# The order of the output projection and the product with the values in each pair step of a fused decoder layer

## What is computed

```python
x = x + attn(layernorm(x), Wq, Wk, Wv, Wr)            # 16 heads of 64, causal penalty -50, scale 1/8
x = x + xattn(layernorm(x), ctx, w_q, w_k, w_v, w_o)  # 16 heads of 64, no mask
x = x + ffn(layernorm(x), ...)                        # swiglu, 8 experts in 2 groups, top 2, and a shared part

# both attentions, per batch row:
scores = einsum('bqhd,bkhd->bhqk', q, k) * scale      # 128 x 128 per head
attn = softmax(scores)
out = einsum('bhqk,bkhd->bqhd', attn, v).reshape(b, s, 1024) @ W_out
```

## Time and profile before

| what | value |
|---|---|
| three timed runs | 966.55, 967.46, 970.04 us; median 967.46 |
| profiled execution, span from the first to the last instruction | 963.6 us |
| TensorE matmuls busy | 932.5 us, 97% |
| TensorE weight loads busy | 806.1 us, 84% |
| VectorE busy | 687.5 us, 71% |
| ScalarE busy | 586.6 us, 61% |
| GpSimd busy | 233.3 us, 24% |
| mean granted clock of TensorE | 0.996 |
| the attention steps (first S to the end of the last step) | 21.9 to about 654 us |

### The profile page before, as it was taken

How to read it: one execution, slowest core, us unless ns; L and a number is a source line. 1 busy time by engine, 2 the same in 40 slices (tenths; PEclk the granted TensorE clock), 3 DMA queues, 4 the chain that set the end, 5 groups by cost and what they waited for, 6 DMA issues and landing times. The chain is left out here.

```text
span 963.6 us, 17001 instructions
## 1 busy us (share of the span) xinstructions
PE 932.5 (97%) x5474; PEld 806.1 (84%) x5474; DVE 687.5 (71%) x1822; ACT 586.6 (61%) x1795; POOL 233.3 (24%) x245
## 2 busy tenths in 40 slices
PE   7999989989999999999999999998899999999998
PEld 6798878878898888888889988986788888888887
DVE  6898878778789878778878877885943554554453
ACT  4988778777788878878878887886501400400400
POOL 1443124214123434422422341344100000000000
PEclk9999999999999999999999999999999999999999
DMA  7300000000001020000000020111100000000000
GB/s 222 107 23 2 1 1 0 0 1 0 0 1 45 23 66 2 1 22 1 0 22 0 0 87 0 44 45 55 56 12 12 0 11 11 0 11 11 1 12 11
DMA packets 13193, 22.12 MB, mean 23 GB/s; under 512 B 1108, under 2 KB 7764, under 8 KB 12628
## 3 DMA queue, kind: packets, MB, share of 16 engines
q1 hardware_dynamic: 13140, 21.51, 6.8%
HBM read 19.41 MB, written 2.10 MB: 22 GB/s over the span
## 5 line engine op out<-in xcount | busy, mean ns | idle before, releaser
L385 POOL TENSOR_TENSOR prob<-prob,rsum 128x512 f32<-128x512 f32 x128 | 133.2, 1040 | 421.1 <-DVE rsum L585 421.1
L466 ACT ACTIVATE prob<-psS,nmin 128x128 f32<-128x128 f32 x512 | 180.9, 370 | 23.3 <-DVE nmin L569 15.9
L554 DVE TENSOR_TENSOR oT_lo<-psT,oT_hi 64x256 fp32r<-64x256 f32 x256 | 108.2, 422 | 16.4 <-ACT oT_hi L454 6.0
L466 ACT ACTIVATION_READ_ACCUMULATOR prob<-psS,nmin 128x1 f32 x512 | 106.5, 208 | 0.0
L448 ACT ACTIVATE pT_hi<-psT 128x512 fp32r<-128x512 f32 x128 | 71.2, 597 | 52.9 <-PE psT L723 52.1
L454 ACT ACTIVATE oT_hi<-psT 64x256 fp32r<-64x256 f32 x256 | 96.6, 377 | 8.5 <-PE psT L124 3.8
L535 DVE TENSOR_TENSOR kd_lo<-psW,kd_hi 64x512 fp32r<-64x512 f32 x128 | 88.0, 687 | 10.4 <-ACT kd_hi L437 6.9
L437 ACT ACTIVATE kd_hi<-psW 64x512 fp32r<-64x512 f32 x128 | 75.9, 593 | 16.4 <-PE psW L124 14.2
L122 PE MATMUL psT<-pT_lo,v_hi 128*128 128x256 f32 x256 | 73.6, 288 | 10.2 <-DVE pT_lo L547 10.1
L547 DVE TENSOR_TENSOR pT_lo<-psT,pT_hi 128x512 fp32r<-128x512 f32 x128 | 82.2, 682 | 1.0 <-ACT pT_hi L448 0.7
L122 PE MATMUL psS<-kd_lo,q_hi 128*128 128x256 f32 x256 | 75.0, 293 | 2.1 <-ACT prob L466 1.1
(11 more groups left out here) (198 smaller groups left out, 2616.4 us busy)
## 6 DMA issues: line engine op xcount, KB each, us to landing
stage<-w SPq DMA_DIRECT2D x4, 1024.0 KB, 4.8
stage<-ctxT SPq DMA_DIRECT2D x4, 512.0 KB, 4.1
out<-fin SPq DMA_DIRECT2D x16, 128.0 KB, 1.7
xres<-x SPq DMA_DIRECT2D x3, 512.0 KB, 8.3
stage<-wq SPq DMA_DIRECT2D x2, 512.0 KB, 5.6
stage<-wk SPq DMA_DIRECT2D x2, 512.0 KB, 6.8
stage<-wv SPq DMA_DIRECT2D x2, 512.0 KB, 5.8
stage<-wr SPq DMA_DIRECT2D x2, 512.0 KB, 4.9
```

Of the source, the lines that this page charges most:

```text
L385: nc.gpsimd.tensor_tensor(prob[:, r, :], prob[:, r, :], rsum[:, r].unsqueeze(2).broadcast_to([P, TPG, P]), ALU.mult).then_inc(prob_done, 1)
L466: e = nc.scalar.activation(prob[:, n, :], flat(psS[:])[:, n * P:(n + 1) * P], ACT.Exp, bias=nmin[:, n:n + 1], scale=-1.0, accum_out=psums[ ...
L554: nc.vector.tensor_tensor(oT[1][r, parity, b, :], banks(psT)[r, b, h, :], oT[0][r, parity, b, :].bitcast(F32), ALU.subtract).then_inc(oT_l ...
```

## The change

The two blocks of calls change places in TensorE's `step`, each with its waits. Nothing else is changed, and no other engine's program.

```diff
@@ -758,12 +758,6 @@
                         pe.wait_ge(gate_in, 32)
                         pe.wait_ge(g_lo, 1)
                         gate_logits(pe, 0)
-                    if depth > 0:
-                        if j == 1:
-                            pe.wait_ge(v_lo, G * 2 * TPG + TPG)
-                        if j == HP + 1:
-                            pe.wait_ge(v_lo, G * 2 * TPG + 2 * TPG)
-                        weighted_values(s, (j - 1) % PAIRS)
                     if depth > 1:
                         if j == 2:
                             pe.wait_ge(res_done, G + 1)
@@ -771,6 +765,12 @@
                         if j == HP + 2:
                             wait_lo(pe, f"{'wx'[sub]}r upper")
                         out_project((j - 2) % PAIRS, j % 2)
+                    if depth > 0:
+                        if j == 1:
+                            pe.wait_ge(v_lo, G * 2 * TPG + TPG)
+                        if j == HP + 1:
+                            pe.wait_ge(v_lo, G * 2 * TPG + 2 * TPG)
+                        weighted_values(s, (j - 1) % PAIRS)
                     if j < TPG:
                         pe.wait_ge(q_lo, s + 2)
                         if j == 0:
```

## The result

The change makes the kernel **slower by 3.6%**: 1001.73 us median (1001.17 to 1002.5, 4 runs) against 968.24 us (966.55 to 970.04, 4 runs: the three of the table and one of 969.01), ratio 1.036 with a 95% interval of 1.034 to 1.038. The forecast was 1003 us. The profiled execution took 1001.17 us, with a span of 999.4 us; the prediction's sum gave a span of 999.1.

The account below looks back on a forecast made before the run. TensorE is busy 97% of the span, but v_lo or prob sets the next projections' start; step costs sum to 35.5 us, taking the span from 963.6 to 999.1 and the median to 1003 us, range 985 to 1015.

Parts of the forecast that it names:

- The slip: First oT_hi on ACT starts 5.20 us after the next pair's projections (QK) start, against 4.29: 0.91 us later.
- threshold of 0.51 us: Room at the first oT_hi: ACT, busy with kd_hi, starts it 0.51 us after TensorE has delivered.
- (b): Step 1, residual ahead of v_lo on DVE: all 0.91 us comes through in six groups, 0.64 in group 4; 6.1 us.
- (c): Steps 4 and 5, no value projection, chain over POOL's prob: 0.91 us in 14 steps, 0.2 in group 3; 12.9 us.
- (d): Step 6: 0.75 us each in groups 0 to 2, nothing in 3 to 6, 0.2 in group 7; 2.5 us.
- (a): Steps 0, 2 and 3, next projections wait for v_lo: 0.27 us in each of 23, plus step 3 adjustments; 6.7 us.
- (e): Step 7, third value tile waits for first tile's v_lo: 0.91 us in groups 3 to 6, 0.8 in 0 to 2; 6.0 us.
- (f): The last step: the output projection's 1.42 us, less 0.15 already waited for pT_lo, comes through; 1.3 us.
- additions for step 3: Self attention, statistics on DVE in step 3: 0.2 us added in groups 0 and 3, 0.35 in 1, 0.25 off in 2.
- fourth rival: A fall of the clock; chance 4%. Its size is not in the text given.
- freed waits: TensorE's waits for pT_lo ahead of the product with the values, at most 10.1 us, counted as giving back nothing.
- The offset: Median of timed runs lies 3.9 us above the profiled span; the same was added to the forecast span of 999.1.

Follow-up runs that it names:

- half-OP kernel: The change with only two of the output projection's four tiles ahead of the product with the values, two behind; 972.96 us, ratio 1.006 against the kernel before.
- halves kernel: The kernel before with the output projection put between the two halves of the product with the values; 966.52 us, ratio 1.000 against the kernel before.

## Why the prediction was right

*The slip.* 5.20 us from QK to oT_hi was forecast and is what the trace shows; the threshold of 0.51 us behind it was hit by the half-OP kernel (0.22 for 0.20), and the halves kernel shows that nothing else about WV's new place matters. Of the signs forecast, ACT's waits for WV (51.1 us for 40 to 55), the wait for pT_lo (5.7 for under 6) and the times from QK to QK (9.58 us from 6.0 for 9.6, 10.67 from 6.1 for 10.6, 0.9 more from 6.4 and 6.5) came.

*The parts.* (b), (c) and (d) came within 0.3 us of their sums, also when tried alone. (a) is right where it is plain: 0.23 to 0.28 us in 13 of the 15 steps 0 and 2, for 0.27. (e) came to 0.83 us a time in groups 3 to 6, not 0.91, and 0.67 for 0.8 in groups 0 to 2. (f) was 1.0 for 1.3. That the sum came so close owes something to luck: -0.9 us at the start, which no part had, and -1.0 in (e) and (f) nearly cancel +1.8 in (a) and +0.4 in (b) and (c). The start is not the change's: in the profiles of the experiments it moves from -0.8 to +1.5 us against the kernel before.

*Where a term was mis-sized.* The additions for step 3 in (a) rest on no row that is shown. In groups 0, 1 and 3 they were near (forecast 0.47, 0.62 and 0.47 us in all, measured 0.38, 0.77 and 0.36). In group 2 0.02 us was forecast and 1.83 measured. TensorE waited there 2.0 us for pT_lo, until 224.89, and from about 1 us behind that wait it ran at a lower clock. Busy time by stretch (us in the stretch, then PE, PEld, DVE, ACT, POOL with counts, and the granted clock):

```profile
225.00:235.00 10.00, 9.12 (x43) 8.06 (x44) 9.25 (x37) 6.24 (x21) 3.25 (x4) 0.66 0.00 1
```

Taken us by us, the granted clock is 0.91 from 225 to 226, 0.50 from 226 to 232, 0.67 from 232 to 233 and 1.00 behind that. The rows of WV's matmuls show it: at 225.24 one lasts 0.28 us and the next starts 0.11 us after it, at 226.24 one lasts 0.41 us and the next starts 0.21 us after it. The later part of WV, V and most of the next S ran at 0.50. The kernel with v_lo ahead of the residual has the change's order in step 3 and a granted clock of 1.00 there (215 to 235 us), and its step 3 of group 2 is 0.18 us shorter than before: so by this comparison 2.0 us of the change's are the clock's. The kernel before had a lower clock in this step too, at 0.83 in its stretch, on WV and OP; it cost about 0.8 us, for the kernel with OP first in steps 6 and 7 alone, with the old order here and a clock of 1.00 from 215 to 225 us, is 0.80 us shorter in it. Outside this step the granted clock is 1.00 throughout the attention steps of the change, with all their pauses of 0.9 us. So a fall of the clock (the fourth rival, 4%) came in one step out of 62, behind a wait of 2.0 us; the mean over the whole run is 0.995, before 0.996.

*The freed waits* were counted at nothing. 4.4 of the 10.1 us went, and the pair of kernels with the exponentials first shows what 8 us of such waits bring once WV's place is free: 0.8 us. TensorE's waits for pT_lo shrank and the time grew: this change brings pT_lo no earlier, it only puts other work into the gap. In the trace the gap lay behind DVE's chain, which the rows on v_lo show.

*Wrong in the list of signs.* ACT's wait before pT_hi was to fall to a third; it fell to 31.5 of 52.1 us. In most of steps 1 to 4 it fell as forecast, from 1.27 to 0.37 us, but ahead of steps 5, 6 and 0 it is what it was, 0.85 and 1.28 us, since there the transposes moved later by as much as ACT did. And the new wait in steps 5 and 6 was named as one for POOL's prob. The idle time that the profile shows is one for the exponentials, a few matmuls earlier (16.0 us; the wait for prob is 1.6). QK still follows POOL's prob by the same 0.53 to 0.54 us, so prob stays the last link of the chain in (c), and the price is the same.

*The offset.* The forecast put the median 3.9 us above the span; for the changed kernel it is 1001.73 - 999.4 = 2.3 us. In each run on record the time lies about 1.8 us above its own span. The rest of the 3.9 came from the kernel before having been profiled in an execution faster than its median. These 1.5 us, and not the sum, are why the median came 1.3 us under the forecast.

What stays open: what decides whether the clock falls in step 3 of groups 1 and 2. The length of the wait for pT_lo alone doesn't: in group 1 a wait of 2.59 us in the kernel before and one of 1.92 us in the change lowered nothing, while in the kernel with OP first in steps 4 and 5 one of 2.59 us stands beside a clock of 0.83. The waits begin on DVE, which stands for 3.6 to 3.9 us with nothing that the profile shows ahead of nmin, where the loop's second and third pass begin (the self attention's loop alone). No run takes this away.

## What to carry to other kernels

When a block is moved on the busiest engine, ask when its consumer asks for it, and what that consumer has queued behind. Here the block had 0.51 us of room, the move took 1.42, and because ACT waited with the exponentials behind it in its order, the whole slip of 0.91 us came back at TensorE in the 20 steps with no other room, and 0.27 us in most of the steps with V. The cheap remedy was on the waiting engine: with what is ready first, the loss was gone (965.04 us for 1001.73). And ask of a visible wait of the busiest engine whether a chain through another engine ends at the same place: here 8 us less of such waits brought 0.8 us.

## What was not expected

A bank that looks free can have another reader. Moving V from the query's bank to the key's bank traded 7 us of waiting for v_lo against 14 us for kd_lo, and left the time within 3 us. And of the two engines that split TensorE's results the less loaded one set the cost: ACT is busy 59% of the span, yet the place of four exponentials in its queue decides some 37 us (1001.73 against 965.04).
